# Two sparse mixtures rewritten: chosen rows fetched by index, the shared branch as a ninth expert, biases as one-row products, sums made in PSUM

## The reference, cut to what matters

```python
sh = _ln(silu(x @ sw1.T + sb1) * (x @ sw2.T + sb2), s_ln_g, s_ln_b)      # hidden width 64
shared_out = sh @ sw3.T + sb3
x_moe = x[index_b, index_t]                                              # 256 chosen tokens
shared_scores = sigmoid(x_moe @ sg_w.T + sg_b)
expert_scores = sigmoid(x_moe @ eg_w.T + eg_b)                           # 8 experts
top1_idx = argmax(expert_scores + exp_bias); top1_score = its expert_score
shared_w, expert_w = softmax([shared_scores, top1_score])
z = _ln(silu(x_moe @ ew1 + eb1) * (x_moe @ ew2 + eb2), sel_ln_g, sel_ln_b)  # all 8 experts
out_all = z @ ew3 + eb3
final_out = shared_out.at[index_b, index_t].set(
    shared_out[index_b, index_t] * shared_w + out_all[top1] * expert_w)
```

## Time and profile before

| | us |
|---|---|
| median of 3 runs | 2433.93 |
| these runs, lowest and highest | 2432.94, 2435.12 |
| the profiled execution, its own time | 2433.29 |
| its span, first to last instruction | 2431.4 |
| PE, DVE, ACT, POOL busy | 2165.6, 1550.0, 1035.3, 145.0 |
| first mixture | 0 to 94.9 |
| second mixture | 554.4 to 630.7 |

### The profile page before, as it was taken

The page is one execution under the profiler, slowest core; times in us unless marked ns, Lnnn a source line. Parts: engine busy times, 40 slices in busy tenths (PEclk is TensorE's granted clock), DMA queues, the critical chain, the costliest instruction groups (busy, mean ns, idle before and its releaser), DMA issues.

```text
span 2431.4 us, 39297 instructions
## 1 busy us (share of the span) xinstructions
PE 2165.6 (89%) x13553; PEld 1354.2 (56%) x13594; DVE 1550.0 (64%) x4432; ACT 1035.3 (43%) x1761; POOL 145.0 (6%) x271
## 2 busy tenths in 40 slices
PE   4569999996699989999999997999999599998698
PEld 3413333334577756566565665777766367775476
DVE  6798888857534346666666665444456735787776
ACT  2126666672234335555554553433333133343133
POOL 5011111115000000000000000000000000000000
PEclk9679999997799989999999998999999789999899
DMA  6010000000000000000000000000100000000000
GB/s 215 13 65 26 25 25 25 25 11 1 1 1 1 1 1 1 1 0 0 0 0 0 0 1 1 1 1 1 55 1 1 0 1 1 1 1 1 1 1 18
DMA packets 20863, 32.04 MB, mean 13 GB/s; under 512 B 5657, under 2 KB 12194, under 8 KB 19970
## 3 DMA queue, kind: packets, MB, share of 16 engines
q1 hardware_dynamic: 20018, 30.12, 3.6%
q10 hardware_dynamic: 720, 0.27, 0.1%
HBM read 25.80 MB, written 4.19 MB: 12 GB/s over the span
## 4 chain that ended last, share of the span: by engine, by line
PE 63%; DVE 9%; ACT 3%; issue 2%; ACTq 0%; DVEq 0%; POOL 0%; POOLq 0%
PE ps L408 19%; PE ps L393 18%; PE ps L604 6%; PE ps L638 5%; PE ps L621 3%; PE ps L588 3%; DVE x L819 1%; ACT arena L736 1%; PE ps L610 1%; PE ps L334 1%; DVE arena L801 1%; PE ps L901 1%; PE ps L256 1%; PE ps L650 1%; PE ps L1055 1%
## 5 line engine op out<-in xcount | busy, mean ns | idle before, releaser
L408 PEld LDWEIGHTS ps<-l_w,arena 128*128 128x128 f32 x4096 | 543.6, 194 | 262.2 <-issue 246.2
L408 PE MATMUL ps<-l_w,arena 128*128 128x128 f32 x4096 | 546.9, 277 | 12.1 <-DVE x L495 10.2
L393 PE MATMUL ps<-xnT,l_w 128*128 128x512 f32 x1024 | 537.8, 609 | 3.3 <-ACT xnT L264 3.3
L495 DVE SCALAR_TENSOR_TENSOR x<-ps,comb,x 128x128 f32<-128x128 f32 x768 | 216.4, 344 | 376.4 <-PE ps L408 374.5
L451 ACT ACTIVATE arena<-ps,l_b 128x512 f32<-128x512 f32 x384 | 263.6, 687 | 410.9 <-PE ps L393 410.8
L1962 DVE TENSOR_REDUCE arena<-ps 128x1 f32<-128x512 f32 x512 | 325.2, 685 | 34.2 <-PE ps L1747 32.2
L1890 ACT ACTIVATE arena<-ps 128x1024 f32<-128x1024 f32 x256 | 252.3, 1022 | 124.7 <-PE ps L1764 124.2
L801 DVE TENSOR_REDUCE arena<-ps 128x1 f32<-128x128 f32 (+7 forms) x256 | 179.0, 751 | 75.8 <-PE ps L610 74.5
L736 ACT ACTIVATE arena<-ps,arena 128x128 f32<-128x128 f32 (+7 forms) x256 | 186.8, 744 | 72.0 <-DVE arena L801 72.0
L1747 PE MATMUL ps<-arena 128*128 128x512 bf16 x480 | 173.6, 394 | 8.3 <-DVE arena L1962 6.0
L744 ACT ACTIVATE arena<-ps 128x512 f32<-128x512 f32 (+1 forms) x192 | 85.4, 489 | 211.6 <-PE ps L621 211.4
(11 more groups left out here) (319 smaller groups left out, 2036.6 us busy)
## 6 DMA issues: line engine op xcount, KB each, us to landing
arena<-s_parts_q SPq DMA_DIRECT2D x96, 48.0 KB
arena<-s_parts_k SPq DMA_DIRECT2D x96, 48.0 KB
l_w<-in_l_w SPq DMA_DIRECT2D x2, 2048.0 KB, 13.9
...
arena<-arena SPq DMA_DIRECT2D x96, 2.0 KB
x<-in_x SPq DMA_DIRECT2D x4, 256.0 KB, 4.2
```

The costliest lines, as they stand in the source:

```text
L393: pe.matmul(k.ps[:, n % 2, :], w.w1[:, e, f * P:(f + 1) * P], k.xnT[:, g * GW:(g + 1) * GW], start=True, stop=True).then_inc(s.hidden_mm.s ...
L408: ins = pe.matmul(k.ps[:, 2 + e % 4, j * P:(j + 1) * P], w.h[:, n % 2, j * P:(j + 1) * P], w.w2[:, e, f, :], start=(f == 0 and j == 0), st ...
L495: ins = dve.scalar_tensor_tensor(k.x[:, t, :], k.ps[:, 2 + e % 4, j * P:(j + 1) * P], k.comb[:, t, e:e + 1], k.x[:, t, :], ALU.mult, ALU.add)
```

## The change

Only the mixtures in first and third place change, and what loads and lays out their arrays.
- **Rows.** The 256 chosen rows of x are fetched from DRAM by two indexed transfers from GpSimd's queue: in the first mixture from the input, in the second from a DRAM copy that SyncE stores as x becomes ready (`l0moe_sync`). They get statistics and a normalization of their own (`slot_stats`, `slot_rows`), and one 256-column transpose and copy. `hot` is gone; `hotT` is made once, in the first mixture, and kept in `arena` for the second.
- **Normalization.** Half of the tiles are normalized by ScalarE.
- **Ninth expert.** The shared branch of the chosen rows is computed beside the eight experts (unit `m`), with the gate (w0 - 1) times 1/count, so that the scattered correction is added to the shared result of all tokens. 1/count comes from the index lists in `number_vector`.
- **Means.** The subtraction of the mean is put into the output weights by a 128 x 128 centring product (`center`), the factor 0.5 as well.
- **Biases.** Each is a product of a row of ones with the bias row that opens the bank's sum, so that silu and the product read PSUM.
- **Order.** Hidden units of 4 x 128 columns (m, e0 to e3, u0 to u3) pass through `silu` and `gated`. The last sums (bias row, scatter, shared branch) stay in PSUM banks 4 to 7, and VectorE adds each once to x.
- **Preparation.** It moves to GpSimd, TensorE and ScalarE, ahead of all products of the first mixture.
- **Loads.** The wide bias tiles become one row each; `center` and a second bias row are added, `tokens` and `score_b` go.

The diff, cut to its core:

```diff
+def spread(dve, st, stat, sm, lo, hi, width, mean=False):
+    mu, rstd, d, v, t = (sm[:, i, lo:hi] for i in range(5))
+    me, mo, se, so = (stat[:, lo:hi, i] for i in (1, 4, 2, 5))
+    if mean:
+        dve.tensor_tensor(mu, me, mo, ALU.add)
+    dve.tensor_tensor(d, me, mo, ALU.subtract)
+    st.done(dve.tensor_tensor(v, se, so, ALU.add))
+    if mean:
+        dve.tensor_scalar(mu, mu, 0.5, None, ALU.mult)
+    st.done(dve.scalar_tensor_tensor(d, d, 0.25, d, ALU.mult, ALU.mult))
+    st.done(dve.scalar_tensor_tensor(v, v, 1.0 / width, d, ALU.mult, ALU.add))
+    st.done(dve.tensor_scalar(v, v, EPS, None, ALU.add))
+    rsqrt(dve, st, v, rstd, t)
+    return mu, rstd
...
+        MX = self.MT * self.NX
+        (self.zu, self.ze, self.zuT, self.zeT, self.z5T, self.xm, self.xmn, self.xmT, self.delta, self.stat, self.sm,
+         self.rt, self.mix, self.gate, self.scale, self.cT, self.nsm) = carve(
+            k.arena, (NT, self.H), (MX, self.H), (NT * self.H,), (self.MT, 4 * P), (self.M,), (self.MT, D),
+            (self.MT, D), (self.M,), (self.MT, D), (NT + MX, 6), (5, NT + MX), (6, MX), (8, self.MT),
+            (self.MT, self.NX), (MX,), (self.M,), (6, NT + self.MT))
...
+def prepare_pool(pool, k, w):
+    pool.wait_ge(w.loaded, w.loads)
+    pool.tensor_scalar(w.ew3g[:, :, :], w.ew3[:, :, :], w.ln[:, 2:3], None, ALU.mult)
+    pool.tensor_scalar(w.sw3g[:, :], w.sw3[:, :], w.ln[:, 0:1], None, ALU.mult)
+    pool.tensor_scalar(w.bsel[:, 0:4, :], w.bmask[:, 0:4, :], w.ln[:, 3:4], 0.5, ALU.mult, ALU.mult)
+    pool.tensor_scalar(w.bsel[:, 4, :], w.bmask[:, 4, :], w.ln[:, 1:2], 0.5, ALU.mult, ALU.mult)
+    pool.tensor_scalar(w.lnh[:, :], w.ln[:, 1:2], 0.5, None, ALU.mult)
+    pool.tensor_scalar(w.B3h[:, :], w.B3[:, :], 0.5, None, ALU.mult)
+    pool.tensor_scalar(w.b3h[0:1, :], w.b3[0:1, :], 0.5, None, ALU.mult).then_inc(w.prep, 1)
...
 def prepare_tensor(pe, k, w):
     pe.wait_ge(w.prep, 1)
+    pe.matmul(k.ps[:, 7, :], w.center[:, :], w.ew3g[:, :, :].rearrange("p q d -> p (q d)"), start=True, stop=True)\
+        .then_inc(w.prep_mm, 1)
...
+    pe.matmul(k.ps[:, 5, 0:D], w.center[:, :], w.sw3g[:, :], start=True, stop=True)
+    for q in range(4):
+        pe.matmul(k.ps[0:NE + 1, 5, D:2 * D], w.bsel[:, q, :], w.ew3[:, q, :], start=(q == 0), stop=False)
+    pe.matmul(k.ps[0:NE + 1, 5, D:2 * D], w.bsel[:, 4, :], w.sw3[:, :], start=False, stop=False)
+    pe.matmul(k.ps[0:NE + 1, 5, D:2 * D], k.ident[0:NE + 1, 0:NE + 1], w.B3h[:, :], start=False, stop=True)
+    pe.matmul(k.ps[0:1, 5, 2 * D:3 * D], w.lnh[0:64, :], w.sw3[0:64, :], start=True, stop=False)
+    pe.matmul(k.ps[0:1, 5, 2 * D:3 * D], k.ident[0:1, 0:1], w.b3h[0:1, :], start=False, stop=True)\
+        .then_inc(w.prep_mm, 1)
...
+def prepare_scalar(act, k, w):
+    act.wait_ge(w.prep_mm, 1)
+    act.activation(w.ew3c[:, :, :].rearrange("p q d -> p (q d)"), k.ps[:, 7, :], ACT.Copy)
+    act.wait_ge(w.prep_mm, 2)
+    act.activation(w.sw3c[:, :], k.ps[:, 5, 0:D], ACT.Copy)
+    act.activation(w.B9[:, :], k.ps[0:NE + 1, 5, D:2 * D], ACT.Copy)
+    act.activation(w.b3c[0:1, :], k.ps[0:1, 5, 2 * D:3 * D], ACT.Copy).then_inc(w.prepared, 1)
...
+def number_vector(dve, st, k, w):
+    dve.wait_ge(w.indices, 16 * 4)
     dve.tensor_copy(w.tmp[:, :], w.ib[:, :])
     st.done(dve.tensor_copy(w.tmpc[:, :], w.ibc[:, :]))
-    dve.scalar_tensor_tensor(w.number[:, :], w.tmp[:, :], float(T), w.it[:, :], ALU.mult, ALU.add)
-    dve.scalar_tensor_tensor(w.numberc[:, :], w.tmpc[:, :], float(T), w.itc[:, :], ALU.mult, ALU.add)\
-        .then_inc(w.numbered, 1)
-    dve.wait_ge(w.numbered, 1)
+    st.done(dve.scalar_tensor_tensor(w.numberc[:, :], w.tmpc[:, :], float(T), w.itc[:, :], ALU.mult, ALU.add))
+    dve.tensor_copy(w.slot[:, :], w.numberc[:, :]).then_inc(w.numbered, 1)
+    st.done(dve.scalar_tensor_tensor(w.number[:, :], w.tmp[:, :], float(T), w.it[:, :], ALU.mult, ALU.add))
+    for m in range(L0Moe.MT):
+        st.done(dve.tensor_scalar(w.tmp[:, :], w.number[:, :], w.numberc[:, m:m + 1], None, ALU.is_equal))
+        st.done(dve.tensor_reduce(w.rc[:, m:m + 1], w.tmp[:, :], AX.X, ALU.add))
+    st.done(dve.reciprocal(w.rc[:, :], w.rc[:, :]))
...
+def l0moe_sync(sp, k, s):
+    for g in range(NG):
+        sp.wait_ge(s.prev, g + 1)
+        sp.dma_start(s.w.rows_out[:, g * GT:(g + 1) * GT, :], k.x[:, g * GT:(g + 1) * GT, :]).then_inc(s.stored, 16)
...
 def l0moe_pool(pool, k, s):
     w = s.w
-    if not s.first:
-        pool.wait_ge(s.norm.rows.sem, s.norm.rows.at(1))
-    pool.wait_ge(w.numbered, 1)
-    for t in range(NT):
-        pool.tensor_scalar(s.hot[:, t, :], w.number[:, :], w.tokens[:, t:t + 1], None, ALU.is_equal)\
-            .then_inc(s.onehot.sem, 1)
+    if s.first:
+        pool.iota(w.iota[:, :], pattern=[[1, NT * P]], base=0, channel_multiplier=0,
+                  allow_small_or_imprecise_dtypes=True).then_inc(w.counted, 1)
+        pool.wait_ge(w.numbered, 1)
+    else:
+        pool.wait_ge(s.stored, 16 * NG)
     for m in range(s.MT):
-        pool.iota(s.hotT[:, m, :], pattern=[[1, NT * P]], base=0, channel_multiplier=0,
-                  allow_small_or_imprecise_dtypes=True).then_inc(s.onehot.sem, 1)
-        pool.wait_ge(s.onehot.sem, s.onehot.at(NT + 2 * m + 1))
-        pool.tensor_scalar(s.hotT[:, m, :], s.hotT[:, m, :], w.numberc[:, m:m + 1], None, ALU.is_equal)\
-            .then_inc(s.onehot.sem, 1)
+        pool.indirect_dma_start(s.xm[:, m, :], None, w.x_in if s.first else w.rows,
+                                bass.IndirectOffsetOnAxis(ap=w.slot[:, m:m + 1], axis=0))\
+            .then_inc(s.gathered[m], 16)
+    if s.first:
+        prepare_pool(pool, k, w)
+        pool.wait_ge(w.counted, 1)
+        for m in range(s.MT):
+            pool.tensor_scalar(w.hotT[:, m, :], w.iota[:, :], w.numberc[:, m:m + 1], None, ALU.is_equal)\
+                .then_inc(w.hot_made, 1)
...
+    def biases(what):
+        bank = s.bank[what]
+        if what == "m":
+            pe.matmul(k.ps[:, bank, 0:2 * P + 18], k.ones[0:1, :], w.slot_b[0:1, :],
+                      start=True, stop=False, skip_group_check=True)
...
+    for what in s.ahead:
+        biases(what)
+    if s.first:
+        turn_slots()
+        for what in ("m", "e0", "e1", "e2", "e3"):
+            hidden(what)
+        pe.wait_ge(w.prepared, 1)
+        turn_rows(0)
+        turn_rows(1)
+        hidden("u0")
+        turn_rows(2)
+        pe.wait_ge(s.mul.sem, s.mul.at(s.at("m")))
+        hidden("u1")
+        turn_rows(3)
+        pe.wait_ge(s.ready.sem, s.ready.at(3))
+        hidden("u2")
+        pe.wait_ge(s.ready.sem, s.ready.at(4))
+        hidden("u3")
+    else:
+        turn_rows(0)
+        turn_rows(1)
+        hidden("u0")
+        turn_rows(2)
+        hidden("u1")
+        turn_rows(3)
+        hidden("u2")
+        hidden("u3")
+        turn_slots()
+        pe.wait_ge(s.mul.sem, s.mul.at(s.at("u1")))
+        hidden("m")
+        hidden("e0")
+        hidden("e1")
+        pe.wait_ge(s.mul.sem, s.mul.at(s.at("u3")))
+        hidden("e2")
+        hidden("e3")
+    pe.wait_ge(s.mul.sem, s.mul.at(s.at("e3")))
...
+    for bank in range(4):
+        pe.matmul(k.ps[:, 4 + bank, :], k.ones[0:1, :], w.b3c[0:1, :].unsqueeze(1).broadcast_to([1, GT, P]),
+                  start=True, stop=False, skip_group_check=True)
+    pe.wait_ge(s.zeT_out.sem, s.zeT_out.at(s.MT + 1))
+    for m in range(s.MT):
+        at = slice(m * P, (m + 1) * P)
+        for q in range(4):
+            pe.matmul(k.ps[:, 3, at], s.zeT[:, m, q * P:(q + 1) * P], w.ew3c[:, q, :], start=(q == 0), stop=False)
+        pe.matmul(k.ps[:, 3, at], s.z5T[0:s.H, at], w.sw3c[0:s.H, :], start=False, stop=False)
+        ins = pe.matmul(k.ps[:, 3, at], s.cT[0:s.NX, at], w.B9[:, :], start=False, stop=True)
...
+    def scatter(q, odd):
+        for j in range(GT):
+            t = 8 * q + 2 * j + odd
+            for m in range(s.MT):
+                pe.matmul(k.ps[:, 4 + 2 * odd + q, j * P:(j + 1) * P], w.hotT[:, m, t * P:(t + 1) * P],
+                          s.delta[:, m, :], start=False, stop=False, skip_group_check=True)
...
+    scatter(0, 0)
+    scatter(0, 1)
+    turn_hidden(0)
+    turn_hidden(1)
+    scatter(1, 0)
+    scatter(1, 1)
+    shared(0)
+    shared(1)
...
+    rows(0)
+    if s.first:
+        slots_out()
+        rows(1)
+        rows(2)
+        rows(3)
+        sigmoid()
+        for what in ("m", "e0", "e1", "e2", "e3"):
+            silu(what)
+        rows_out(0)
+        rows_out(1)
+        exps()
+        silu("u0")
+        rows_out(2)
+        silu("u1")
+        rows_out(3)
+        silu("u2")
+        silu("u3")
+    else:
+        rows(1)
+        rows(2)
+        rows(3)
+        rows_out(0)
+        rows_out(1)
+        silu("u0")
+        rows_out(2)
+        silu("u1")
+        rows_out(3)
+        silu("u2")
+        silu("u3")
+        slots_out()
+        sigmoid()
+        for what in ("m", "e0", "e1", "e2", "e3"):
+            silu(what)
```

(91 more changed lines are left out.)

444 lines of the change are left out of this document (221 added, 223 removed).

## The result

The changed kernel takes 2414.26 us, the median of 4 runs (2413.39 to 2415.12), against 2433.65 of the kernel before in the same comparison (4 runs, 2432.94 to 2435.12): the ratio is 0.9915, with a 95% interval of 0.9899 to 0.9931. That is 19.4 us less where 35.9 were forecast. The execution that was profiled took 2413.39 us, with a span of 2411.2.

The account below looks back on a forecast made before the run. No engine was taken as full: each of the two mixtures is a chain passing between engines. Shorter chains save 18.3 + 17.6 = 35.9 us, so 2433.9 - 35.9 = 2398; range 2384 to 2416, own range 2392 to 2404.

Parts of the forecast that it names:

- rival A: Closing chain of both mixtures: TensorE's clock stays at half, 7.4 us more a stage, 2413; chance 20%.
- step 8: End of each mixture: output-bias rows 6.5 us, starting at half clock, then twelve small products 2.9; first mixture to 60.0.
- Step 9: After the small products: copy, scatter products, transposes and shared-branch products, 10.7 us; first mixture to 70.7.
- Step 10: VectorE's closing steps of each mixture, 5.9 us; first mixture ends at 76.6.
- The covers: First mixture, GpSimd's two comparisons beside VectorE's row statistics: counted nothing, hidden behind TensorE's preparation and bias rows; worst case 31.5.
- Steps 1 to 3: Front of first mixture: weights landed 16.0, GpSimd's seven scalings 4.3 us to 20.3, TensorE's preparation 5.8 us to 26.1.
- Step 4: First mixture, TensorE's bias rows ahead of the chosen rows: 4.2 us, to 30.3.
- Step 5: First mixture, two transposes of chosen rows and a 256-column copy: done at 31.0 with the hops.
- Steps 6 and 7: First mixture: ScalarE's row tiles, table loads, sigmoid, first silu to 35.6; then VectorE's units, statistics, gates, products to 50.6.
- The second mixture's gather: x written out, then read back by GpSimd's two gathers: landed at 562.4, range 561 to 569.
- Rival B: Loads and gathers become the bound: 19.9 and 569, +10.5 us at most, 2403 to 2409; chance 15%, the port two thirds.
- Rivals C and D: C: each gather costs GpSimd 10.2 us beyond 1.0, slower, 3%. D: about 30 us of new waits, 2%.

Follow-up runs that it names:

- 5: Changed kernel with only the hidden layers' bias rows as products with 128 rows instead of one: 2409.7 us.
- 6: Changed kernel with all bias rows, hidden layers' and output, as products with 128 rows instead of one: 2396.3 us.
- experiment 4: Changed kernel, first mixture: GpSimd's two comparisons after the rows' normalization, chosen rows transposed ahead of the experts' bias rows, which stay one-row: 2427.3 us.
- experiment 8: Changed kernel with all bias rows at 128 rows, GpSimd's comparisons late and chosen rows transposed ahead of the experts' bias rows: 2389.5 us.
- experiment 3: Changed kernel with GpSimd's two comparisons of the first mixture waiting until VectorE has normalized its last rows: 2412.2 us.
- 7: Changed kernel with all bias rows at 128 rows and GpSimd's two comparisons late, TensorE's order unchanged: 2392.4 us.
- experiment 1: Changed kernel with only the four output-bias products given 128 rows instead of one: 2401.1 us.

## Why the prediction was right and wrong

The range and the sign held; the point was 16 us too low, and rival A, with its 2413, is in the main what happened. That its number meets 2414 so closely is in part luck. Of the 15.7 us by which the span missed, what rival A named makes 12.9 where it had set 14.8: its bias rows were put at 7.8 us and took 5.3 and 7.1. Later starts of step 8 (3.0 and 1.3 us), for which the clock is not the cause rival A named, make up for it.

- **Step 8 of each mixture is the one that failed**, in what it set for the clock. Its bias rows took less than put, 5.3 us instead of 6.5, from a start 3.0 us late (58.95 measured at their end, 57.1 forecast). But then the clock was to be full: the twelve small products took 7.0 us instead of 2.9 in either mixture. The forecast assumed that 5.4 us of back-to-back work raises the clock, as in the earlier trace rows, and rival A's "no row shows a long run of one-row products" was the right doubt. The pairs that differ in the rows of the biases, 5 and 6 at this very place (0.50 and 1.00 behind the products), 4 and 8 in front (0.50 and 0.97), show that here the rows decide whether it comes back. The start of step 8 was put at half clock because TensorE would have little to do from 36 to 47; it was busy for all of these 11 us and came to the bias rows at 1.00.
- **The terms for a product** in the sum are times of the earlier trace rows and not where the prediction failed: 3.81/16 = 0.24 us for 128 columns at a granted clock of 0.98, 2.08/4 = 0.52 at 0.50; 3.70/4 = 0.93 for 512 columns at 1.00, and twice the pass of 0.98 (2.93 for three), 1.95, at 0.50. That a one-row product costs as its columns do was the author's estimate; experiment 4 has 2.07 us for one and 2.08 for its like with 128 rows.
- **Step 9** inherits this: from the small products' end to the last shared product 13.8 us instead of 10.7, 3.0 of it in the first 32 scatter passes (6.64 against 3.6). Step 10 was 5.0 instead of 5.9.
- **The covers** counted nothing for GpSimd's comparisons beside VectorE's statistics. They cost: steps were held four times, and the spread took 9.2 us more than in experiment 3. The chosen rows were ready at 31.7, past the worst case of 31.5, though the loads were 2.2 us earlier than in step 1 and GpSimd's work 2.6 earlier than in step 2. Experiments 3 and 7 price the cover at 4 us of the first mixture. "Up to 3.6 us per comparison" was too little, and the traces show why: it depends on which step meets the comparison. Steps with one input were held to the comparison's end: the 1.69 above, and in experiment 1, whose comparisons ran from 19.32 to 30.19, two that filled them both:

```profile
18.67 6.12 DVE L118 TENSOR_SCALAR arena<-arena 128x18 int32<-128x18 int32 x1
24.83 5.39 DVE L119 TENSOR_SCALAR arena<-arena 128x18 int32<-128x18 int32 x1
```

Steps with two inputs were let through 3.7 to 3.8 us after the comparison's start, with the rest of its 5.4 us still to run: the 3.38 and 3.66 above, and the 3.58 of the earlier trace rows. (The 1.40 above has two inputs too, but stood behind a one-input step that was held until 23.17.) Why the two kinds differ no run shows.
- **Steps 1 to 3** came early (GpSimd starts at 13.8, its work ends at 17.7, TensorE's preparation at 22.9 where 16.0, 20.3 and 26.1 were put). **Step 4** took 6.3 us instead of 4.2, again the clock (0.85 and then 0.50, above), but it ended at 29.2, before the chosen rows, and cost nothing. Step 5, whose own terms add up to 31.2 and not 31.0, ended at 32.8: the hold minus the early loads. **Steps 6 and 7** ended 2.6 and 3.0 us late; ScalarE's six row tiles in step 6 took 2.4 us instead of 1.5.
- **The second mixture's gather** was put at 562.4; shifted by the 9.3 us that the mixture now starts earlier, 553.1. It was there at 551.1. Rival B didn't show. What its chance calls the port, that VectorE's row steps hold GpSimd's gather off, was a guess that no run bears out: GpSimd's second gather is issued at 548.65, VectorE's row steps run beside it from 548.70, and it landed after 2.4 us, the first one after 2.6. Rivals C and D are out with it, a gather costing GpSimd 0.95 to 1.14 us. The bias rows of step 8 began 1.3 us later than forecast and took 7.1 us instead of 6.5; small products 4.1 and scatter 2.3 us longer, closing steps 0.9 shorter, make the rest of the 7.4 us by which the end was missed.
- **The stages between** gained or lost under 2 us: the full stage is 0.9 longer, in the experiments up to 3.5 (461.4, experiment 8). This stays unexplained.

The sum, first mixture: +3.0 up to the last unit, -1.2 bias rows, +4.1 small products, +3.1 scatter, -0.9 closing steps, which is the 8.1 between 84.7 and 76.6.
